# A recurrent ODE solver with an FFN woven into it: other slots for the FFN's work, and tanh ahead of the square on ScalarE

## The reference

```
dq = q - q**3 / 3 - p + drive + tanh(q) @ coupling.T + bias
dp = EPSILON * (q + ALPHA - BETA * p)
q_next, p_next = clip(q + DT/6*(dq1 + 2*dq2 + 2*dq3 + dq4)), clip(p + ...)
```

## Time and profile before

| what | value |
|---|---|
| median of 3 runs | 1735.76 us (1735.63 to 1736.38) |
| the profiled execution | 1733.82 us, of which the span of its instructions is 1732.0 us |
| mean granted TensorE clock | 0.975 of full speed |
| busy in the span | TensorE 90%, its weight loads 55%, VectorE 65%, ScalarE 29%, GpSimd 22% |
| GRU and attention, up to the scan's first transpose | 1077 us |
| the scan with the FFN in it, to its last new state | 609 us |
| the FFN's drain behind it | 46 us |

### The profile page before, as it was taken

How to read it: one execution, slowest core, us unless ns; L and a number is a source line. 1 busy time by engine, 2 the same in 40 slices (tenths; PEclk the granted TensorE clock), 3 DMA queues, 4 the chain that set the end, 5 groups by cost and what they waited for, 6 DMA issues and landing times.

```text
span 1732.0 us, 45724 instructions
## 1 busy us (share of the span) xinstructions
PE 1551.0 (90%) x16744; PEld 951.5 (55%) x16744; DVE 1126.0 (65%) x3319; ACT 507.8 (29%) x1589; POOL 380.3 (22%) x554
## 2 busy tenths in 40 slices
PE   5999899999859999999999998788888888888884
PEld 2333333333738576675767753556666666666662
DVE  2888743333786475664747541568888888888885
ACT  1233211112120202102020110355555555555552
POOL 1222010000000000000000000235555555555554
PEclk9999999999969999999999998999999999999997
DMA  7322210005000000000000005101111111111111
GB/s 303 79 76 61 79 29 12 12 11 111 1 0 1 25 0 24 6 18 23 1 24 0 24 6 184 42 23 29 33 31 44 35 35 33 30 33 30 42 35 35
DMA packets 88432, 70.27 MB, mean 41 GB/s; under 512 B 30728, under 2 KB 80824, under 8 KB 87352
## 3 DMA queue, kind: packets, MB, share of 16 engines
q1 hardware_dynamic: 86616, 63.75, 12.7%
q0 software_dynamic: 1760, 5.77, 1.2%
HBM read 52.55 MB, written 16.92 MB: 40 GB/s over the span
## 4 chain that ended last, share of the span: by engine, by line
PE 69%; DVE 14%; issue 8%; ACT 5%; DMA 2%; POOL 1%; SPq 1%; ACTq 0%; DVEq 0%; POOLq 0%
PE ps L681 13%; PE ps L671 13%; PE ps L775 10%; PE ps L588 9%; PE ps L596 9%; PE ps L715 3%; PE ps L765 2%; PE ps L739 2%; ACT mem L964 2%; DVE mem L1317 2%; DVE mem L1275 2%; ACT ps L956 2%; PE ps L692 1%; PE ps L789 1%; PE ps L585 1%
## 5 line engine op out<-in xcount | busy, mean ns | idle before, releaser
L775 PE MATMUL ps<-mem 128*32 128x128 f32 x8192 | 280.7, 278 | 89.7 <-ACT mem L964 85.6
L775 PEld LDWEIGHTS ps<-mem 128*32 128x32 f32 x8192 | 212.8, 111 | 165.2 <-ACT mem L964 118.3
L671 PE MATMUL ps<-mem 128*128 128x512 f32 x512 | 224.6, 593 | 0.0
L681 PE MATMUL ps<-mem 128*128 128x256 f32 x1024 | 222.3, 379 | 0.0
L681 PEld LDWEIGHTS ps<-mem 128*128 128x128 f32 x1024 | 194.2, 190 | 25.8
L514 POOL TENSOR_TENSOR mem<-mem 128x128 f32<-128x128 f32 x64 | 30.7, 480 | 784.7 <-ACT mem L959 784.5
L588 PE MATMUL ps<-mem 128*32 128x384 f32 x2048 | 181.5, 496 | 0.0
L596 PE MATMUL ps<-mem 128*32 128x384 f32 x2048 | 179.0, 491 | 2.7 <-DVE mem L1122 2.7
L671 PEld LDWEIGHTS ps<-mem 128*128 128x128 f32 x512 | 95.7, 190 | 109.6 <-issue 109.2
L518 POOL TENSOR_TENSOR mem<-mem 128x128 f32<-128x128 f32 x192 | 101.2, 527 | 171.8 <-ACT mem L959 165.7
L765 PE MATMUL ps<-mem 128*128 128x128 f32 x768 | 138.6, 304 | 0.0
(11 more groups left out here) (129 smaller groups left out, 2104.8 us busy)
## 6 DMA issues: line engine op xcount, KB each, us to landing
mem<-x_scr SPq DMA_DIRECT2D x128, 64.0 KB, 1.8
mem<-in_xT SPq DMA_DIRECT2D x64, 64.0 KB, 1.8
mem<-in_Wq SPq DMA_DIRECT2D x1, 4096.0 KB
mem<-in_Wo SPq DMA_DIRECT2D x1, 4096.0 KB
mem<-in_x SPq DMA_DIRECT2D x16, 256.0 KB, 2.7
x_scr<-mem SPq DMA_DIRECT2D x32, 128.0 KB, 2.3
q_scr<-mem SPq DMA_DIRECT2D x64, 64.0 KB, 1.6
mem<-q_scr SPq DMA_DIRECT2D x64, 64.0 KB, 1.9
```

The costliest lines, as they stand in the source:

```text
L671: mm = pe.matmul(ps[:, 6 + pr, :], aoT[:, h, pr * P:pr * P + P], wo[:, h, :], start=(h == 0), stop=(h == HEADS - 1))
L681: mm = pe.matmul(ps[:, h % Q_BANKS, 0:BLK], wq[:, c, h * DH:(h + 1) * DH], xnb[:, c, :], start=(c == 0), stop=(c == NC - 1))
L775: mm = pe.matmul(ps[32 * j:32 * j + 32, st % 2, 0:P], thT[:, c, :], ct[:, c, j * P:(j + 1) * P], start=False, stop=(c == NC - 1), skip_gro ...
```

## The change

Seven edits. (1) ScalarE: in stages 1 to 3, tanh's two halves run ahead of the square, as in stage 0. (2) ScalarE: the scaled `q` tile moves from k 6 to 4, silu from k 12, 13, 0, 2 to 13, 14, 1, 3, the copies of transposes from k 1, 4 to 0, 5. (3) VectorE: the sum of drive and bias moves from stage 2 to stage 0 of each step. (4) VectorE: largest value, scale and reciprocal of the `q` tile all stand in k 3; the scale is written to a tile of its own (`xnew`) and copied into `xsx` in k 8. (5) VectorE: the largest value of `t` is taken in four quarters of 352 in k 1, 2, 5, 6, in place of two halves in k 3, 6. (6) VectorE: the scale of `t` moves from k 7 to the end of k 6. (7) ScalarE's two waits ahead of its groups are gone. GpSimd, TensorE and SyncE keep their order.

```diff
@@ act stage
-                if st:
-                    squared()
                 for half in range(2):
                     act.wait_ge(rk_qT, 2 * n + half + 1)
                     act.activation(thT[:, 2 * half:2 * half + 2, :], qsT[:, 2 * half:2 * half + 2, :], ACT.Tanh).then_inc(rk_th, 1)
+                squared()
                 if st == 0:
-                    squared()
                     wait_if(act, rk_pa, 4 * t - 3)
@@ act slot
-                    if k == 6:
+                    if k == 4:
                         act.wait_ge(f_rq, i + 1)
...
-                    if k in (12, 13):
-                        silu_part(i, k - 12)
+                    if k in (13, 14):
+                        silu_part(i, k - 13)
...
-                    if k in (0, 2):
+                    if k in (1, 3):
                         silu_part(i, 2 + k // 2)
...
-                    if k == 1:
+                    if k == 0:
                         t_kept(i, 0)
-                    if k == 4:
+                    if k == 5:
                         t_kept(i, 1)
-
-            act.wait_ge(ct_ld, 16 * 4)
-            act.wait_ge(rk_bits, 1)
@@ dve stage
                 fill()
-                if st == 2 and not end:
+                if st == 0 and not (last and s == 3):
                     drive_sum(t + 1, (s + 1) % 4, g + 1 + (s == 3))
@@ dve slot
-                    if k == 5:
+                    if k == 3:
                         dve.wait_ge(q_ld, 16 * TILE_T * (i + 1))
-                        v.did(dve.tensor_reduce(xam, qt, AX.X, ALU.max, apply_absolute_value=True))
-                    if k == 6:
-                        v.need(v.n)
-                        if tile(1) is not None:
-                            dve.wait_ge(f_gated, GU_T * tile(1) + GU_T)
-                        v.need(v.did(dve.tensor_scalar(xsx, xam, 1.0 / FP8_MAX, None, ALU.mult)))
-                        dve.reciprocal(xrs, xsx).then_inc(f_rq, 1)
+                        v.need(v.did(dve.tensor_reduce(xam, qt, AX.X, ALU.max, apply_absolute_value=True)))
+                        v.need(v.did(dve.tensor_scalar(xnew, xam, 1.0 / FP8_MAX, None, ALU.mult)))
+                        dve.reciprocal(xrs, xnew).then_inc(f_rq, 1)
...
+                    if k == 8:
+                        if tile(1) is not None:
+                            dve.wait_ge(f_gated, GU_T * tile(1) + GU_T)
+                        v.did(dve.tensor_copy(xsx, xnew))
                     if k in (12, 13):
+                        if k == 12:
+                            v.need(v.n)
                         gate_part(i, k - 12)
...
-                    if k in (3, 6):
-                        half = k // 6
-                        dve.wait_ge(f_gated, GU_T * i + 2 * half + 2)
-                        v.did(dve.tensor_reduce(tam2[:, half:half + 1], tt[:, half * 2 * GU_N:(half + 1) * 2 * GU_N], AX.X, ALU.max,
-                                                apply_absolute_value=True))
-                    if k == 7:
+                    if k in (1, 2, 5, 6):
+                        m = (1, 2, 5, 6).index(k)
+                        dve.wait_ge(f_gated, GU_T * i + m + 1)
+                        v.did(dve.tensor_reduce(tam4[:, m:m + 1], tt[:, m * GU_N:(m + 1) * GU_N], AX.X, ALU.max, apply_absolute_value=True))
+                    if k == 6:
                         v.need(v.n)
-                        v.need(v.did(dve.tensor_reduce(tam, tam2, AX.X, ALU.max)))
+                        v.need(v.did(dve.tensor_reduce(tam, tam4, AX.X, ALU.max)))
```

More of the change, by code:

```diff
@@ L85 @@
 T_PARTS = ((0, 6 * P), (6 * P, INNER))
-GROUP_STEPS = 12
+GROUP_STEPS = 15
 def wait_if(eng, sem, value):
@@ L264, in gru_attn_rk4_ffn @@
         yout = f32(w.take(D), D)
-        tam2 = f32(w.take(2), 2)
-        tam, tsx, tsy, trs, xam, xsx, xrs = (f32(w.take(1), 1) for _ in range(7))
+        tam4 = f32(w.take(4), 4)
+        tam, tsx, tsy, trs, xam, xnew, xsx, xrs = (f32(w.take(1), 1) for _ in range(8))
         (wih_ld, whh_ld, w_att, b_ld, c_ld, xt_ld0, xt_ld1, h0_ld, st_ld, wg_ld, wu_ld, idx_ld, wd_ld, x_ld, x1_wr, q_ld, x1_ld,
```

## The result

The changed kernel takes 1804.25 us (median of 4 runs, 1802.15 to 1809.27), against 1735.7 before: a ratio of 1.040, 95% interval 1.0376 to 1.0424. It is **slower by 4%**. The span of its profiled execution is 1800.9 us, against 1732.0.

What follows compares the result with a forecast made beforehand. Waits, not a full engine, bound the scan: VectorE waiting for ScalarE's square and the coupling matmuls. Terms of 5.6 - 2.4 - 0.3 + 0.2 + 1.9 gave +5.0 us a group, +68 in all: 1804 us, range 1770 to 1821.

Steps and rivals of the forecast that it cites:

- Today's square is free: ScalarE, stages 1 to 3: tanh waits for a transpose until 0.61 us anyway, so moving it ahead gains nothing.
- The wait ahead of L1308, +5.6: VectorE: the later square delays L1308 from 0.64 to 1.22 us in stages 1 to 3; +5.6 us a group.
- The wait for the matmuls, -2.4: VectorE ahead of L1317: the wait for the coupling matmuls, 2.55 us a group, nearly goes; -2.4.
- The meetings with GpSimd, +1.9: L1285 held behind L536 in k 12, L1407 delaying L518 and the next seed L1294; +1.9 us a group.
- The reductions, 0.42 to the next instruction: VectorE: each quarter reduction of 352 takes 0.42 us; four replace two of 0.80, +0.1 a group.
- k 8 as before, -0.3 for the earlier scaling and k 11: GpSimd's L548 sets k 8, so freed ScalarE gains nothing there; earlier scaling and shorter k 11 wait give -0.3 a group.
- The groups: Whole program: groups 3 to 15 +65 us, group 2 +3, group 1 +1, group 0 nothing, drain -1; together +68.
- A: Rival: VectorE's order costs as forecast, but GpSimd's chain does not meet L1285 or L1407; 1779 us, chance 0.25.
- B: Rival: TensorE's granted clock falls to 0.96, about 1.3 us more a group; 1821 us, chance 0.06.
- C: Rival: faster, since edit 2 empties ScalarE's queue, which holds VectorE, and the late square costs nothing; 1721 us, chance 0.05.
- D: Rival: no change, ScalarE's freer slots give back what the late square costs; 1736 us, chance 0.02.
- A flip of k 8: In k 8 VectorE's L1395 goes ahead of GpSimd's L548, sparing about 0.8 us a group, 10 us in all; 1793.

Runs made afterwards that it cites:

- slots_only: The changed kernel without edits 1 and 3, leaving the new slots (edits 2, 4, 5, 6, 7): 1717.54 us, a group of 36.55.
- slots_qT_in_11: slots_only with ScalarE's copy of the turned `q` tile moved from k 10 to k 11, behind tanh: 1701.68 us, a group of 35.67.
- after_bias_in_psum: The changed kernel with the bias kept in PSUM, so L1285 reads one SBUF and one PSUM input: 1789.51 us, a group of 41.76.

## Why the prediction was right, point by point

The forecast was 1804 us with a group of 43.0; measured 1804.25 and 42.94. So close a hit is partly luck, as the parts show.

- *"Today's square is free"*, and tanh gains nothing: shown. Tanh starts at 0.60 in either order, released by the transpose.
- *The wait ahead of L1308, +5.6*: the start moved by 0.57, as worked out; the wait itself grew from 2.75 to 7.5, +4.75, 0.9 less than the sum had. I had priced each stage by the move of the start (0.58), while the row of the wait gives 0.51: 0.06 of it had been overlap of neighbouring instructions, which costs the stage as much but is no idle time. *The wait for the matmuls, -2.4*: it went to nothing, -2.55. Alone, edit 1 cost 3.5 a group where these two terms gave 3.2.
- *The meetings with GpSimd, +1.9*: k 12 at 4.11 where 4.1 was worked out, L1289 of k 0 and k 12 at 1.01 after the new state where 1.02 was. The mechanism is shown by the run with the bias in PSUM, which is worth 1.2 a group.
- *The reductions, 0.42 to the next instruction*: 0.51 long, 0.43 to the next. As chosen.
- *k 8 as before, -0.3 for the earlier scaling and k 11*: k 8 took 3.63 against 3.53. k 11 took 0.63 less, but k 10 gave that back, and edit 1 alone does the same. Without edits 1 and 3 the reason given for k 8 ("the gain has no outlet") was wrong: there, as far as the rows of slots_only show, the earlier scaling put L1393 ahead of L548, and k 8 lost 1.16.
- *The groups*: from group 3 to group 15 the scan took 62.3 us more, where I had 65. Group 2 cost 5.5 more instead of 3: in k 9 to k 11 the granted clock fell to the lower of its two levels (1.2 of 2.4 GHz), behind gaps of 1.27 and 2.04 us in TensorE's work, the 32 matmuls took 1.94 instead of 1.08, and k 11 took 4.87. Group 1 and the drain, +1 and -1 expected, cost 0.5 and 0.2. These errors cancelled. The stretch with the low clock:

```profile
1178.00:1190.00 12.00, 9.66 (x122) 7.24 (x126) 6.74 (x23) 3.72 (x18) 4.08 (x6) 0.57 0.01 1
```

Gaps alone do not tell when the clock falls. In group 2, k 9, the 32 matmuls of slots_only took 1.93 us, behind gaps of 1.15 and 1.56 us; those of slots_qT_in_11 took 1.08, behind gaps of 1.14 and 1.57.

The terms do not simply add, which the prediction had not said, and here the sum was luckier than its parts. Taken in the order edit 1, new slots, edit 3, the runs give +3.5, +0.8 and +0.6 us a group (41.52, 42.30, 42.94); the prediction had +3.2, -0.1 and +1.9. The new slots by themselves give -1.5. From the four corners of edits 1 and 3, the new slots kept in all: edit 3 costs 3.0 us a group with the square early (36.55 to 39.53), but 0.6 with it late (42.30 to 42.94); edit 1 costs 5.75 with the sum in stage 2 and 3.4 with it in stage 0. With the square late, L1285 meets a GpSimd operation in either place (L536 or L529); with it early, only in stage 0 (L536, and L548 in k 8).

Of the rivals, A (1779) fell on k 12. Half of its condition, L1285 not held, was run as after_bias_in_psum and came to 1789.5; the other half, L1407 ahead of L518, stays there (k 0 at 2.94). B fell in the loop, clock 1.00 at 33 us of work in 43, and had one episode in group 2. C was right about one thing only: edit 2 does free ScalarE, and without edits 1 and 3 the slots are worth 16 us. D fell.

A flip of k 8, which I had put at 10 us, did not come in the changed kernel and did come in slots_only, where k 8 is 1.16 a group shorter. In the loop it is decided by less than a tenth of a microsecond: VectorE's mask (L1395 before, L1391, L1393) starts 0.06 behind L548 before, 0.07 behind it in the changed kernel, 0.04 ahead of it in slots_only. In the changed kernel the mask had gained as much on its stage as in slots_only (1.89 into it, instead of 1.99), but L548 too came 0.11 earlier. In the written-out groups 2 and 15 of slots_only it is no close race: L548 starts 0.43 ahead, and k 8 takes 3.09. The order could be made firm by a wait; that was not tried.

## What to carry to other kernels

An instruction that waits in an in-order queue costs what stands behind it, not what it does itself: before moving a producer later, look at its consumer's queue. Moving work ahead of another's helps only if it could have started earlier; see what released it first. And a few hundredths of a microsecond (0.06 behind or 0.04 ahead) decided here whether VectorE or GpSimd went first, and that was worth 1.16 us of a group; where a small VectorE operation has two SBUF inputs, holding one operand in PSUM took it out of GpSimd's way.

## What the runs showed of the hardware that I had not expected

L1285 was held by GpSimd only when both of its inputs were in SBUF: 1.44 us against 0.28 with one of them in PSUM, at the same half microsecond into a GpSimd operation of 1.8. The prediction had the first half of this from one row; the second half is what the run added. It is not the whole condition, though: L1395, a mask of 128x768 with a single input, is held in the same way, and what sets it apart was not tested.

Who comes first goes through at its own length, and the other waits for nearly all of the rest: L548 1.27 when first, 1.65 behind a VectorE operation that had started 0.04 earlier; that operation 0.55 in front, 1.61 to 1.63 behind. Adding the held instruction's own length to what was left of the other gives 0.13 us more than was measured, each time: 1.57 against 1.44 for L1280 behind L536, 1.76 against 1.63 for L1395 behind L548, 1.78 against 1.65 for L548 behind L1393, 1.10 against 0.97 for L1280 behind L529.
